# A two-layer graph attention kernel: the second layer's mask added by VectorE with the row maxima, the first layer's exponentials in SBUF, the attended rows kept in PSUM

## The reference, cut to what matters

```python
# layer 0: relational attention (8 heads of 32), then a feed-forward net
attn = softmax(q @ k.T / sqrt(dh))                       # per head
out = sum(((attn * (adj == r)) @ v_r) for r in range(4)) # one set of values per edge type
x1 = ln(src + out @ Wo + bo);  x2 = ln(x1 + gelu(x1 @ W1 + b1) @ W2 + b2)
# layer 1: masked attention with a leaky relu on the scores
e = q @ k.T;  e = where(e >= 0, e, 0.2 * e)
h = softmax(where(adj > 0, e, -9e15)) @ v
out = layernorm(concat([layernorm(h), x2]) @ Wffn.T) + x2
```

## Time and profile before

| | |
|---|---|
| runs of the kernel (3): median, lowest to highest | 2408.63 us, 2406.07 to 2409.92 |
| the profiled execution: its time / its span in the trace | 2403.04 us / 2401.2 us |
| TensorE's granted clock, mean | 0.989 of full speed |

### The profile page before, as it was taken

The page is one execution under the profiler, slowest core; times in us unless marked ns, Lnnn a source line. Parts: engine busy times, 40 slices in busy tenths (PEclk is TensorE's granted clock), DMA queues, the critical chain, the costliest instruction groups (busy, mean ns, idle before and its releaser), DMA issues.

```text
span 2401.2 us, 80726 instructions
## 1 busy us (share of the span) xinstructions
PE 2284.4 (95%) x30284; PEld 1850.1 (77%) x30284; DVE 2115.4 (88%) x3987; ACT 2120.3 (88%) x5976; POOL 1698.0 (71%) x1870
## 2 busy tenths in 40 slices
PE   2799999999999999999999999999999999999984
PEld 1577888788788788788788887877877877877863
DVE  3779999999999999999999999999999998998973
ACT  4689999998999999999899999999999999999973
POOL 1467777777777777777777777777777777777763
PEclk9999999999999999999999999999999999999997
DMA  4447557657667666756756765766665675675553
GB/s 132 87 89 141 106 115 137 113 110 133 115 112 130 121 111 124 129 110 117 138 107 115 138 114 109 133 120 106 130 125 107 124 132 109 115 142 103 108 99 67
DMA packets 948549, 280.53 MB, mean 117 GB/s; under 512 B 877249, under 2 KB 947393, under 8 KB 948161
## 3 DMA queue, kind: packets, MB, share of 16 engines
q1 hardware_dynamic: 944992, 271.95, 61.0%
q10 hardware_dynamic: 3168, 3.41, 0.5%
HBM read 40.38 MB, written 16.78 MB: 24 GB/s over the span
## 4 chain that ended last, share of the span: by engine, by line
PE 56%; ACT 6%; DMA 6%; SPq 3%; issue 3%; DVE 2%; POOL 1%; DVEq 0%; ACTq 0%; POOLq 0%
PE bank L523 43%; PE bank L621 6%; PE bank L584 4%; DMA pT<-p1h 3%; ACT bank L778 3%; DMA xT<-x_rows 2%; PE bank L602 1%; SPq L477 1%; SPq L470 1%; ACT p0h L849 1%; ACT p L767 1%; SPq L427 1%; POOL x_rows L1178 1%; PE bank L554 1%; PE bank L569 1%
## 5 line engine op out<-in xcount | busy, mean ns | idle before, releaser
L973 DVE TENSOR_TENSOR pm<-pT,bank 128x4096 f16<-128x4096 f16 x256 | 573.4, 2277 | 9.8 <-DMA pT<-p0h 9.4
L523 PE MATMUL bank<-wv,xT 128*128 128x512 f16 (+1 forms) x2304 | 449.6, 345 | 0.0
L778 ACT ACTIVATE bank<-bank,p_nmax 128x128 f32<-128x128 f32 x1024 | 355.8, 369 | 23.9 <-DVE p_nmax L959 19.4
L1178 POOL TENSOR_TENSOR h<-h_f,h 128x512 f16<-128x512 f32 x256 | 292.6, 1164 | 96.6 <-ACT h L754 96.5
L523 PEld LDWEIGHTS bank<-wv,xT 128*128 128x128 f16 x2304 | 220.8, 98 | 178.3 <-issue 18.2
L523 PE MATMUL bank<-yT,w 128*128 128x256 f16 x3072 | 356.7, 273 | 0.3 <-DMA yT<-x_rows 0.2
L523 PE MATMUL bank<-w,h 128*128 128x256 f16 x3072 | 345.7, 272 | 2.7 <-POOL h L1178 2.7
L1178 POOL TENSOR_TENSOR x_rows<-x,x_rows 128x512 f16<-128x512 f32 x128 | 148.2, 1157 | 270.2 <-ACT x_rows L821 157.6
L767 ACT ACTIVATE p<-p,p_nmax 128x128 f32<-128x128 f32 x1024 | 336.5, 435 | 0.8
L523 PEld LDWEIGHTS bank<-yT,w 128*128 128x128 f16 x3072 | 295.3, 98 | 41.8 <-issue 0.8
L523 PEld LDWEIGHTS bank<-w,h 128*128 128x128 f16 x3072 | 295.9, 98 | 36.2 <-issue 2.8
(11 more groups left out here) (125 smaller groups left out, 4888.6 us busy)
## 6 DMA issues: line engine op xcount, KB each, us to landing
x_sb<-in_x_dram SPq DMA_DIRECT2D x64, 256.0 KB, 3.0
adj_i<-in_adj_dram SPq DMA_DIRECT2D x128, 128.0 KB, 2.7
out_dram<-x2b SPq DMA_DIRECT2D x64, 256.0 KB, 3.0
xT<-x_rows SPq DMA_TRANSPOSE x128, 3.2
pT<-p0h SPq DMA_TRANSPOSE x128, 4.6
oT<-o_rows SPq DMA_TRANSPOSE x128, 3.2
pT<-p1h SPq DMA_TRANSPOSE x128, 5.0
pm<-in_L_gnn_W_dram ACTq DMA_DIRECT2D x1, 1024.0 KB, 13.1
```

Of the source, the lines that this page charges most:

```text
L523: last = nc.tensor.matmul(o, l, r, start=(first and k == 0), stop=(final and k == len(todo) - 1))
L778: last = nc.scalar.activation(ps(f"s0_{r}")[:, at:at + P], ps(f"s0_{r}")[:, at:at + P], ACT.Exp, bias=p0_nmax[:, r, g, c:c + 1], accum_out ...
L973: V_.tensor_tensor(pm0[g][:, s], pT0[g][:, s].unsqueeze(1).broadcast_to([P, REL, HEADS, P]), edges[:, g].unsqueeze(2).broadcast_to([P, REL ...
L1178: return V_.tensor_tensor(to, source, high, ALU.subtract)
```

## The change

The mask no longer goes through TensorE. `max_1` becomes sixteen operations on VectorE, one for each r, graph and column block, that add the mask (now float32, in the place of `adj1_i`) to a 128 by 128 piece of the scores in PSUM, write the sum to `p1` and put out its row maximum; the leaky relu then runs in place in SBUF, once on `p1` and once on the maxima (`leaky_max_1`), and `negated_max_1` negates these. `exp_0` writes to two buffers `p0` in SBUF, and `probs_low_0` moves to GpSimd. The attended rows of the second layer stay in PSUM until `attention_normed_1` writes `o1`. Banks, lags and the order of every engine's steps are written anew. Cut to its core (the tables of banks and the lists of steps are left out; where they matter the program's rows stand below):

```diff
...
-    ("s1_0", 4, 3, "s1_leaky", 4, 1),
+    ("s1_0", 6, 3, "p1_max", 4, 1),
...
-    ("s0_0", 7, 0, "p0_lo", 4, 1),
+    ("s0_0", 6, 0, "p0_exp", 4, 1),
...
-        neg_mask = sb("neg_mask", [G, P], BF16)
+        neg_mask = adj1_i[:].bitcast(F32)
...
+        p0 = [sb(f"p0_{u}", [G, C, P]) for u in range(2)]
...
-        o0_lo = sb("o0_lo", [G, D])
+        o0_lo = sb("o0_lo", [D])
...
                 def scores_1(m):
...
-                    pe.wait_ge(S["adj1_mask"], m + 1)
-                    for r in range(ROWS):
-                        nc.tensor.matmul(ps(f"s1_{r}")[:], ident16[:], neg_mask[:].unsqueeze(2).broadcast_to([P, G, C, P]),
-                                         start=True, stop=False)
...
                 def leaky_1(m, r):
-                    act.wait_ge(S["s1_ps"], m + 1)
...
+                    act.wait_ge(S["p1_max"], 4 * m + r + 1)
+                    rows = p1[:, r].rearrange("p g c j -> p (g c j)")
+                    nc.scalar.activation(rows, rows, ACT.Prelu, alpha=ALPHA).then_inc(S["s1_leaky"], 1)
+
+                def leaky_max_1(m):
+                    act.wait_ge(S["p1_max"], 4 * m + 4)
...
+                    nc.scalar.activation(p1_lmax[:], p1_max[:], ACT.Prelu, alpha=ALPHA).then_inc(S["p1_lmax"], 1)
...
                 def exp_1(m, r):
-                    act.wait_ge(S["p1_max"], 4 * m + r + 1)
+                    act.wait_ge(S["p1_nmax"], m + 1)
+                    act.wait_ge(S["s1_leaky"], 4 * m + r + 1)
...
                 def exp_0(m, r):
...
+                    if past(4 * m + r - 1):
+                        act.wait_ge(S["p0_lo"], 4 * m + r - 1)
...
-                            last = nc.scalar.activation(ps(f"s0_{r}")[:, at:at + P], ps(f"s0_{r}")[:, at:at + P], ACT.Exp,
+                            last = nc.scalar.activation(p0[r % 2][:, g, c], ps(f"s0_{r}")[:, at:at + P], ACT.Exp,
...
                 def max_1(m, r):
-                    dve.wait_ge(S["s1_leaky"], 4 * m + r + 1)
...
+                    dve.wait_ge(S["s1_ps"], m + 1)
+                    dve.wait_ge(S["adj1_mask"], m + 1)
...
+                    for g in range(G):
+                        for c in range(C):
+                            at = (g * C + c) * P
+                            last = V_.tensor_tensor_reduce(out=p1[:, r, g, c], in0=ps(f"s1_{r}")[:, at:at + P], in1=neg_mask[:, g],
+                                                           scale=1.0, scalar=LOWEST, op0=ALU.add, op1=ALU.max,
+                                                           accum_out=p1_max[:, r, g, c:c + 1])
+                    last.then_inc(S["p1_max"], 1)
+
+                def negated_max_1(m):
+                    dve.wait_ge(S["p1_lmax"], m + 1)
...
+                    V_.tensor_scalar(p1_nmax[:], p1_lmax[:], -1.0, None, ALU.mult).then_inc(S["p1_nmax"], 1)
...
                 def rows_in(name, g):
 
-                    return o1[:, g] if name == "o1" else ps(name)[:, g * D:(g + 1) * D]
+                    return rows_and_sum(g)[:, :, 0:DH] if name == "o1" else ps(name)[:, g * D:(g + 1) * D]
...
+                def probs_low_0(m, r):
+                    pool.wait_ge(S["p0_hi"], 4 * m + r + 1)
+                    low(p0h[:, :, 1, :, r], p0[r % 2][:], p0h[:, :, 0, :, r]).then_inc(S["p0_lo"], 1)
...
```

More of the change, by code:

```diff
@@ L81 @@
              "o1_rstd", "oT1_lo", "p1_lo", "w_eps", "w_rstd", "x2_plus_b",
+             "p0_lo",
              "xT0_lo",
@@ L164, in build @@
         h = sb("h", [2, FC, T], F16)
-        x2 = [sb(f"x2_{u}", [G, D]) for u in range(2)]
+        x2 = [sb(f"x2_{u}", [G, D]) for u in range(X2R)]
         v1 = sb("v1", [2, G, HEADS, DH + 1], F16)
@@ L539, in transpose_rows @@
                             at = (c * G + g) * P
-                            last = nc.tensor.transpose(o[:, at:at + P], src[:, g, c * P:(c + 1) * P], ident[:])
+                            last = nc.tensor.transpose(o[:, at:at + P], src[:, g, c * P:(c + 1) * P], ident)
                     return last
@@ L1108, in steps @@
                     if live(n - 1):
-                        values_low_0(n - 1, 0)
-                    if live(n - 2):
-                        residual_0(n - 2)
-                        statistics("y0", n - 2)
-                    if live(n - 1):
-                        recip_0(n - 1)
-                    if live(n - 2):
-                        aggregate("y0", n - 2)
-                        centred_gained("y0", g1_row, n - 2)
-                        rows_x1(n - 2)
-                    if live(n - 4):
-                        max_1(n - 4, 3)
+                        values_low_0(n - 1, 3)
+                        by_edge_type(n - 1, 0, 0)
+                        by_edge_type(n - 1, 0, 1)
+                        by_edge_type(n - 1, 1, 0)
+                        by_edge_type(n - 1, 1, 1)
+                        attention_added_0(n - 1, 0)
                     if live(n - 5):
@@ L1149, in steps @@
                         aggregate("o1", n - 4)
[L1150 to L1152 removed]
+                    if live(n - 2):
+                        no_edge(n - 2)
                     if live(n - 1):
[L1154 removed]
+                        residual_0(n - 1)
                     if live(n):
                         max_0(n, 2)
[L1157 to L1160 removed]
                     if live(n - 4):
                         attention_normed_1(n - 4)
[L1163 to L1164 removed]
+                    if live(n - 1):
+                        statistics("y0", n - 1)
+                    if live(n - 3):
+                        negated_max_1(n - 3)
+                    if live(n - 1):
+                        aggregate("y0", n - 1)
+                    if live(n):
+                        max_0(n, 3)
+                    if live(n - 1):
+                        centred_gained("y0", g1_row, n - 1)
+                        rows_x1(n - 1)
+                    if live(n - 2):
+                        residual_ff(n - 2)
+                        statistics("f", n - 2)
+                        aggregate("f", n - 2)
+                    if live(n - 3):
+                        values_low_1(n - 3)
+                    if live(n - 2):
+                        centred_gained("f", g2_row, n - 2)
+                    if live(n):
+                        values_low_0(n, 0)
+                        values_low_0(n, 1)
+                        values_low_0(n, 2)
                 pipeline(steps)
```

416 lines of the change are left out of this document (199 added, 217 removed).

## The result

The changed kernel takes 2444.89 us (median of 4 runs, 2443.36 to 2448.18) against 2409.09 us of the kernel before on the same chip: ratio 1.0154, 95% interval 1.0138 to 1.0171. It is slower, where 2374 us had been forecast. The profiled execution took 2443.36 us, its span is 2441.4.

A forecast was written before the change was run, and what follows sets the result against it. TensorE was taken to bound the steady step, before and after. From the profiled 2403.0 us, 37.8 less over 59 steps and 3.5 more in the drain gave 2368.7; the runs' median lies 5.6 above, so 2374 us, range 2341 to 2428.

The forecast's parts named there:

- TensorE's sum, 34.34 a step: TensorE's work in a steady step: 35.20 us less 0.86 for the four mask matmuls of `scores_1`.
- a steady step costs TensorE's own 35.20 and 0.38 of disturbance: Kernel before: its 35.58 us mean step is TensorE's busy time plus 0.38 in steps where it waits for DMA transposes.
- VectorE, 32.4: VectorE's busy time a step after the change, 27.8 + 16p us, with p taken as 0.29.
- p: VectorE's spacing of one masked maximum, main instruction plus read of the maximum: 0.28 to 0.46 us, taken as 0.29.
- The rivals with p = 0.42 and 0.46: VectorE: main instruction at half rate, 2414 us, chance 0.08; pair without overlap, 2452 us, chance 0.17.
- ScalarE 33.5 and GpSimd 31.0: Busy times a step after the change: ScalarE 32.81 + 0.7, GpSimd 26.47 + 4.52 us; both said to fit.
- GpSimd in its order: Rival: GpSimd keeps 3 us of its idle time and becomes the bound at 35.5 us, about 2407 us, chance 0.08.
- So I raise the mean disturbance from 0.38 to 0.60: Allowance per step, in us, for TensorE's waits, raised because the ring and two other covers are thin.
- the ring: One pair's chain through the engines from the second `attend_0`, a floor for the step: 28.9 + 16p, 33.5 us at 0.29.
- thin covers: `scores_0` has some 0.2 us over the copies of k0 and q0, the second `attend_0` some 0.4 over `by_edge_type`.
- the forecast step of 34.94: Mean step after the change, 34.34 + 0.60 us, against 35.58 before: 59 steps save 37.8 us.
- The drain, 3.5: Second layer's first exponential waits once for all sixteen maxima instead of a group of four: 12p = 3.5 us more.

The follow-up runs named there:

- mask_back: `loads_x2` plus four matmuls of the old mask matmuls' size ahead of the second layer's scores, output unchanged: 2441.67 us, ratio 1.0140.
- before_no_mask: The kernel before with the four mask matmuls of `scores_1` left out and nothing else: 2415.07 us, ratio 1.0023.
- loads_x2: The changed kernel with SP issuing x and adj0 loads a step earlier, behind `load_adj1`, and x2's transpose ahead of x's: 2392.32 us, ratio 0.9930.
- low_dve: The changed kernel with the four low halves of p0 (`probs_low_0`) back on VectorE instead of GpSimd: 2457.27 us, ratio 1.0209.
- x1_early: `loads_x2` with the rows of x1 ahead of p0's last quarter on ScalarE and GpSimd, their transpose ahead of p0's on SP: 2454.05 us, ratio 1.0193.

## Why the prediction was wrong

Point by point:

- **TensorE's sum, 34.34 a step: right.** The best step takes 34.33, and `mask_back` prices the four matmuls at 0.79 a step in the new order. Half wrong was the view behind it, that in the kernel before "a steady step costs TensorE's own 35.20 and 0.38 of disturbance": a second chain lay right behind, and `before_no_mask` gained nothing.
- **VectorE, 32.4: right in kind, 1 us too high.** p is 0.21, below the lower bound of 0.28: the read's 83 ns lie wholly beside the next main one. 27.8 + 16 x 0.21 = 31.2; the negation takes 0.74 instead of 0.15, the mask of `no_edge` 0.28 instead of 0.58. Measured 31.43. The rivals with p = 0.42 and 0.46 fell. The Trainium skill's Vector Engine (DVE) Microarchitecture Reference (Points that are easy to get wrong) names half rate for a scalar-tensor-tensor operation with two SBUF sources that are not bf16. Here, with one source in PSUM, the main one takes 286 ns, against 285 worked out at full rate: nothing contradicts the page, and no run here tries two SBUF sources.
- **ScalarE 33.5 and GpSimd 31.0: right**, 33.37 and 30.92. GpSimd in its order did not become the bound: it has some 5 us of idle time a step, and waits for ScalarE ahead of the rows of x1.
- **"So I raise the mean disturbance from 0.38 to 0.60": the step that failed.** It is 35.91 - 34.33 = 1.58, of which 1.15 is waits of TensorE; most of the rest is TensorE's own busy time, 34.70 on average against 34.33, which no run explains. The prediction looked for thin covers along the ring, at `scores_0` and `attend_0`; the thin ones were those of the transposes of x2 and x1, in SP's queue, where `load_x` and the transpose of x, as before ahead of that of x2, now fall into a stretch without a pause. The prediction looked at the cover of a transpose only for p0 and p1, and made no walk of SP's queue. Against the forecast step of 34.94 that is 0.97 x 59 = 57 us. The runs give back 53 us by SP's order alone, and in `loads_x2` the mean excess is 35.06 - 34.33 = 0.73, close to the 0.60 forecast.
- **The fill, not mentioned, hence at nothing: 16.45 us.** The forecast counted 59 steps and the drain. What the runs exclude: SP's loads, the low halves on GpSimd (202.11 and 202.66) and the granted clock. What they show: with the two last maxima of VectorE ahead of the residual the first bias matmul came at 199.77, where nine runs with that part as in the changed kernel lie between 202.11 and 204.08; the times cannot confirm these 2.3 us (ratios 0.9921 and 0.9930, with intervals that overlap). Early queries add nothing to that: with them it came at 207.95, 206.26 and 200.79. That the rest comes from the new order of several engines together, by which one pair's attended rows stand inside the next pair's chain, is argued from the rows and not shown; it stays open.
- **The drain, 3.5: near, in part by luck.** It is 4.4, but with the measured p the forecast's own term is 12 x 0.21 = 2.5; the rest was not traced.

57.2 + 16.45 + 0.9 is the 74.5 us by which the span missed the forecast (40.2 more instead of 34.3 less); the medians missed by 71.

## What to carry to other kernels

A saving on the busiest engine is worth only what the next chain lets through: leave the work out first, and see whether the time falls at all. When an order is written anew, walk each in-order DMA queue as an engine of its own: what is ready when, what is issued ahead of it, and how much cover its consumer has; here one load of 0.91 us a step cost 39 us, and moving it to a quiet place brought the change from 1.5% slower to the time of the kernel before (ratio 0.9986), and with its neighbours to 0.7% faster. The load need not be new: ahead of the same transpose it delayed nothing in most steps while the queue still had pauses. And count the fill as a term of its own: here it is 16.45 of the 40.2 us by which the span grew.

## What the runs showed of the hardware that was not expected

- VectorE's negation of 128x16 elements in SBUF takes 744 ns on average in the changed kernel (the group above, L975). In `low_dve`, where GpSimd idles at that point, it takes:

```profile
L974 DVE TENSOR_SCALAR p_nmax<-p_lmax 128x16 f32<-128x16 f32 x64 | 10.5, 165 | 0.0
```

  In the changed kernel a low half of p0 is running on GpSimd when 58 of the 64 negations begin, and each of these ends 0.03 us after that low half, however long it has to wait; the other 6 take 157 to 167 ns. The Trainium skill's SBUF — State Buffer (SBUF: two separate sides) describes an exclusive lock between GpSimd and certain VectorE operations on a shared pair of ports. The trace agrees with that.
- A masked maximum, add and maximum with its read, is spaced 0.21 us at 128 float32 elements: the accumulator's read cost nothing.
- A DMA transpose was slower in company: x1's lands after a median of 3.2 us ahead of those of p0 (`x1_early`), 3.9 between them (`loads_x2`). SP's issue of the two transposes of x and x2 took 4.10 us in the step shown, but 2.67 in the median of the steady steps of the changed kernel and 2.66 in `loads_x2`: the load ahead of them does not make them longer.
